# Third norm ahead of the matrix memory's norms, maxima of the second attention ahead of router, context mean and context sum

## What is computed

```
x = _layernorm(x + _L0_attn_ref(x, ...))            # first norm
x = _layernorm(x + _L0_xattn_ref(x, ctx, ctx, ...)) # matrix memory, a norm of its own inside; second norm
x = _layernorm(x + _L0_ffn_ref(x, ...))             # router, top 2 of 8 experts and a shared one; third norm
x = _layernorm(x + _L1_attn_ref(x, ...))            # second attention, 16 heads of width 8
x = _layernorm(x + _L1_xattn_ref(x, ctx, ...))      # uses the context's mean over the tokens
x = _layernorm(x + _L1_ffn_ref(x, ...))
```

## Time and profile before

| | |
|---|---|
| timed runs | 2484.64, 2486.62 and 2490.05 us; median 2486.62 |
| the profiled execution | 2482.89 us, of which 2481.2 are the span from first to last instruction |
| mean granted clock of PE | 0.901 of full speed |
| busy share of the span | PE 78%, DVE 68%, PEld 55%, ACT 45%, POOL 34% |
| chain that ended last | DVE 36%, PE 36%, issue 14%, POOL 6%, ACT 4%, DMA 2% |

### The profile page before, as it was taken

The page is one execution under the profiler, slowest core; times in us unless marked ns, Lnnn a source line. Parts: engine busy times, 40 slices in busy tenths (PEclk is TensorE's granted clock), DMA queues, the critical chain, the costliest instruction groups (busy, mean ns, idle before and its releaser), DMA issues.

```text
span 2481.2 us, 41883 instructions
## 1 busy us (share of the span) xinstructions
PE 1933.4 (78%) x14136; PEld 1373.1 (55%) x14136; DVE 1675.4 (68%) x3985; ACT 1113.2 (45%) x3168; POOL 842.6 (34%) x775
## 2 busy tenths in 40 slices
PE   2785697778886888678877888679877888775698
PEld 1464366645674457545664467546664567554354
DVE  8895894679656993669556993779466983713355
ACT  2462365335642465336642565246542564232234
POOL 0552462317420651226321651236321651211000
PEclk8997899889996999799997999799987999687699
DMA  4000012201040013101030203001120203051000
GB/s 136 1 1 9 15 54 64 64 18 61 5 121 12 28 41 93 42 13 58 23 105 11 68 1 114 21 15 56 56 71 11 69 1 118 10 200 61 9 13 21
DMA packets 72770, 117.35 MB, mean 47 GB/s; under 512 B 7822, under 2 KB 46870, under 8 KB 72038
## 3 DMA queue, kind: packets, MB, share of 16 engines
q1 hardware_dynamic: 67014, 101.42, 12.7%
q0 software_dynamic: 5536, 13.12, 1.8%
HBM read 95.18 MB, written 18.81 MB: 46 GB/s over the span
## 4 chain that ended last, share of the span: by engine, by line
DVE 36%; PE 36%; issue 14%; POOL 6%; ACT 4%; DMA 2%; DVEq 0%; SPq 0%; POOLq 0%; ACTq 0%
PE bank L1355 34%; DVE work L495 11%; DVE bank L504 5%; DVE work L513 3%; DVE work L493 3%; DVE max L794 2%; POOL hid L1263 2%; ACT work L952 2%; PE bank L1359 1%; POOL work L1231 1%; POOL work L1243 1%; DMA hid<-y_sorted,slot_id 1%; DVE acc L712 1%; ACT hid L952 1%; PE bank L1500 1%
## 5 line engine op out<-in xcount | busy, mean ns | idle before, releaser
L1355 PEld LDWEIGHTS bank<-work 128*128 128x128 f32 (+2 forms) x5152 | 389.6, 204 | 186.6 <-issue 146.6
L1355 PE MATMUL bank<-work 128*128 128x128 f32 (+2 forms) x5152 | 422.2, 312 | 69.3 <-DVE max L794 42.4
L952 ACT ACTIVATE work<-bank 128x512 f32<-128x512 f32 (+1 forms) x560 | 246.7, 516 | 317.1 <-PE bank L1355 264.8
L495 DVE TENSOR_TENSOR work<-bank,table_space 64x512 f32<-64x512 f32 x512 | 352.2, 688 | 6.8
L1231 POOL TENSOR_TENSOR work<-work 128x512 f32<-128x512 f32 x128 | 163.4, 1277 | 368.1 <-DVE work L495 267.7
L952 ACT ACTIVATE work<-work 128x512 f32<-128x512 f32 (+1 forms) x338 | 196.6, 618 | 166.8 <-DVE work L581 77.4
L952 ACT ACTIVATE work<-work,negmax 128x128 f32<-128x128 f32 x512 | 199.0, 390 | 100.2 <-DVE negmax L515 100.2
L1238 POOL TENSOR_TENSOR work<-sb_ident,nrm 128x512 f32<-128x512 f32 x128 | 133.2, 1041 | 275.4 <-ACT nrm L952 275.4
L1355 PE MATMUL bank<-work,table_space 128*128 128x512 f32 x256 | 140.4, 630 | 89.9 <-DVE negmax L515 59.4
L952 ACT ACTIVATE hid<-bank,w_ring 128x128 f32<-128x128 f32 x480 | 136.4, 370 | 162.9 <-PE bank L1355 162.8
L493 DVE TENSOR_TENSOR work<-bank,table_space 128x512 f32<-128x512 f32 x256 | 173.9, 679 | 45.2 <-PE bank L1355 19.2
(11 more groups left out here) (287 smaller groups left out, 3426.0 us busy)
## 6 DMA issues: line engine op xcount, KB each, us to landing
w_ring<-in_w_routed SPq DMA_DIRECT2D x120, 514.0 KB, 4.1
x_quad<-x_sorted SPq DMA_DIRECT2D x24, 256.0 KB, 2.9
y_sorted<-y_quad SPq DMA_DIRECT2D x24, 256.0 KB, 2.5
x_T<-in_x_T POOLq DMA_DIRECT2D x9, 256.0 KB, 3.1
x_row<-in_x_row POOLq DMA_DIRECT2D x9, 256.0 KB, 4.6
ctx_T<-in_ctx_T SPq DMA_DIRECT2D x8, 256.0 KB, 2.6
work<-in_ctx_row SPq DMA_DIRECT2D x8, 256.0 KB, 2.9
out<-act_row SPq DMA_DIRECT2D x8, 256.0 KB, 2.3
```

The lines of the kernel that those rows point to most:

```text
L495: last = v.tensor_tensor(rows(wk[i + 1][o]), rows(src[p]), sinT[o, s].unsqueeze(1).broadcast_to([DH0, GB, N]), ALU.mult)
L952: return nc.scalar.activation(o, i, f, **k)
L1355: return nc.tensor.matmul(o, l, r, start=start, stop=stop, skip_group_check=True)
```

## The change

On DVE the application of the third norm (`norm_t`) moves up, ahead of the product into `act_row[1]`; `scale_q2` moves ahead of the application of the second norm; the mean `cbc` and `context_sum` move behind `router_choice`; and `router_softmax` moves from ahead of `attn1` to behind the first four maxima. On ACT `t_to_T` moves ahead of the memory's norm and `mask_k2` ahead of the second norm. On PE the transposes of the third norm go to bank 6 and no longer to bank 3, which is still being read then; `wv2` waits for the statistics of the memory's norm (its bank 2 is free by then); and the transposes of `tok` and the router's logits move behind `scores2(0)`. POOL's and SP's programs stay as they are.

```diff
@@ DVE, xattn
                 link(v.reciprocal(rden[:], den[:]))
+                if d:
+                    dve.wait_ge(stored, g * 32 + 16)
+                    norm_apply(norm_t, g, 0, acc, act_row[0])
                 hr = act_row[1][:].rearrange("p b (h d) -> p b h d", h=H1)
...
                 norm_stats(norm_x, act_row[1])
-                if d:
-                    dve.wait_ge(stored, g * 32 + 16)
-                    norm_apply(norm_t, g, 0, acc, act_row[0])
                 norm_apply(norm_x, g, 1, act_row[1], resid_x, ahead=d)
...
-                norm(norm_x, g, 2, resid_x, tok, ahead=d)
+                norm_stats(norm_x, resid_x)
                 if d:
                     scale_q2(g)
+                norm_apply(norm_x, g, 2, resid_x, tok, ahead=d)
@@ DVE, attn1
-                v.tensor_scalar(cbc[:], csum[:].unsqueeze(2).broadcast_to([128, GB, N]), 1.0 / N, None,
-                                ALU.mult).then_inc(ctx_mean, 1)
-                if more:
-                    dve.wait_ge(ctx_mean, g + 1)
-                    context_sum()
-
...
                         v.tensor_reduce(max2[:, :, n, r], rows(ring2[(4 * n + r) % 6]), X, ALU.max).then_inc(mx2, 1)
+                    if n == 0 and more:
+                        router_softmax(g, 1)
...
                     router_choice(g, 1)
+                v.tensor_scalar(cbc[:], csum[:].unsqueeze(2).broadcast_to([128, GB, N]), 1.0 / N, None,
+                                ALU.mult).then_inc(ctx_mean, 1)
+                if more:
+                    dve.wait_ge(ctx_mean, g + 1)
+                    context_sum()
                     sort_tokens(g, 1)
@@ ACT, xattn
                     norm(norm_t, g, 0)
+                    t_to_T(g, 0, bank[6])
                 norm(norm_x, g, 1, ahead=d)
                 if d:
-                    t_to_T(g, 0, bank[3])
+                    mask_k2(g)
                 norm(norm_x, g, 2, ahead=d)
-                if d:
-                    mask_k2(g)
@@ PE, project2
-                transposes(bank[3], act_row[0], t_tr)
+                transposes(bank[6], act_row[0], t_tr)
...
+                if beside_norms:
+                    pe.wait_ge(norm_x.stats, g * LNS + LNS + 2)
                 for b in range(GB):
                     last = mm(rows(bank[2])[:, b], rows(seq_T)[:, b], res["wv2"][:], start=b == 0)
@@ PE, attn1
                 scores2(0)
+                if more:
+                    tokens_T(g, 1)
+                    router_logits(g, 1)
                 scores2(1)
```

More of the change, by code:

```diff
@@ L837, in _ @@
             xattn(0, 1)
-            router_softmax(0, 1)
             attn1(0, True)
@@ L843, in _ @@
                 xattn(g, 1)
-                router_softmax(g, 1)
                 attn1(g, True)
@@ L1178, in _ @@
             norm(norm_t, G - 1, 0)
-            t_to_T(G - 1, 0, bank[3])
+            t_to_T(G - 1, 0, bank[6])
             mask_k2(G - 1)
@@ L1615, in gate_tot_columns, with project2 @@
                 gate_columns(bank[0], gate[3], gate_T)
-            def project2(g):
+            def project2(g, beside_norms):
                 pe.wait_ge(norm_t.out, g * LNS + 1)
-                transposes(bank[3], act_row[0], t_tr)
+                transposes(bank[6], act_row[0], t_tr)
                 pe.wait_ge(t_T_sb, g * LNS + 1)
@@ L1655, in xattn, with tokens_T, router_logits @@
                         last.then_inc(num, 1)
-                if d:
-                    project2(g)
+            def tokens_T(g, d):
                 pe.wait_ge(norm_x.out, tally(g, d, LNS, 3))
                 transposes(bank[6], tok, x_tr)
+            def router_logits(g, d):
                 pe.wait_ge(x_T_sb, tally(g, d, 2, 2))
@@ L1785, in _ @@
             xattn(0, 0)
+            tokens_T(0, 0)
+            router_logits(0, 0)
             token_ranks(0, 0)
@@ L1790, in _ @@
             xattn(0, 1)
+            project2(0, True)
             attn1(0, 2, True)
@@ L1795, in _ @@
                 xattn(g, 1)
+                project2(g, True)
                 attn1(g, g + 2, True)
             heads_and_experts(G - 1, 1, False, True, True)
-            project2(G - 1)
+            project2(G - 1, False)
             attn1(G - 1, G, False)
```

## The result

The changed kernel takes 2493.97 us, median of 11 runs (2491.27 to 2497.9); the kernel before, beside it, 2487.73 (2483.95 to 2492.84, 11 runs). The ratio is 1.0025, with a 95% interval from 1.0016 to 1.0034: 6.2 us slower. The prediction drew the line between no change and slower at 0.2%; the median lies just past it, and the interval reaches to both sides of it. The profiled execution took 2491.27 us (span 2489.5, mean granted clock 0.898) against 2482.89 before (2481.2, 0.901).

A forecast was written before the change was run, and what follows sets the result against it. DVE's router, mean, sum and maxima set the stage's end, POOL's v2 chain 0.68 us behind; afterwards v2 binds. Net 0.12 us a group, 7 x 0.12 = 0.8 us, on the median 2486.62 gave 2487.4, range 2479 to 2495.

The forecast's parts named there:

- The bound after the change: Second scores: they wait for ACT's v2 copies behind POOL's memset and tok, no longer for maxima; 0.12 us later a group.
- the first rival, the clock: Behind the second scores PE's clock rises later in some groups (2495, chance 0.18) or earlier (2477, chance 0.08).
- the sum alone: Second scores 0.12 us later in each of seven groups, 0.8 us in all; bounds 0.4 to 2.8.
- The third rival, the maxima setting the pace: Second scores follow the earlier maxima and start 4.6 us sooner a group, 32 us in all: 2454; chance 0.05.
- Tok: Last norm's output on DVE, held by q2's scaling, ends 0.75 us later than before.
- Covers: ACT's seq_T and k2 copies end 0.22 and 0.14 us before the logarithms; mean and sum fit DVE's rank wait: cost 0.
- ACT's queue, the second rival: k2 copies ahead of the last norm's root delay tok by up to 2.40 us a group, 17 in all: 2504; chance 0.07.
- from ACT's end to PE's start: Between ACT's last v2 copy and PE's second scores: 0.05 us, within the 767.24 against 767.12 forecast for their start.
- more late rises: Behind the second scores three short groups turn long, 3 x 2.6 = 7.8 us, with the 0.8 2495; chance 0.18.

The follow-up runs named there:

- swapped waits: Changed kernel with PE's wait for the maxima put ahead of those for k2 and v2 before the second scores: 2494.26 us against 2487.2 for the kernel before.
- plain delay: Kernel before with two small DVE operations added ahead of the maxima of each group but the last: 2496.98 us against 2489.87.
- mean in front: Changed kernel with context mean and sum put back ahead of the maxima: 2496.91 us against 2489.87 for the kernel before.
- third norm alone: Kernel before with third norm, seq_T, q2, k2 and bank 6 edits only; mean, sum, router and maxima in old order: 2496.84 us against 2489.87.
- longest delay: Kernel before with four small DVE operations added ahead of the maxima of each group but the last: 2500.92 us against 2487.2, 4 runs.
- v2 cleared first, before: Kernel before with POOL's memset of v2 moved up behind a first quarter of moe_bias: 2486.56 us, ratio 0.9997.
- both edits: Kernel before with mean and sum behind the router's choice and POOL's memset of v2 behind a first quarter of moe_bias: 2447.33 us against 2488.17.

## Why the prediction was right and wrong

**The bound after the change: right.** The measured 2493.97 lies inside the range only because that took in the first rival, the clock; the sum alone was bounded at 2.8 us above before. The bound itself came as predicted. The prediction let the maxima off the path and put POOL's chain behind tok in their place. ACT's copies release the second scores, the maxima wait 5.67 us, and clearing v2 sooner takes the changed kernel to 1.1% below the kernel before and does nothing in the latter. The third rival, the maxima setting the pace, is out.

**Tok: right within 0.06 us.** Predicted 0.75 later, measured 0.81 (9.79 - 8.98). The bare root wait is the 0.60 that was read off the other norm, and tok stands right behind q2, as worked out. The third norm starts 0.48 us behind the reciprocal's start where `act_row` had stood 0.39 behind it; those 0.09 are more than the 0.06 left over. From tok to the end of the copies 7.22 us were measured for 7.23.

**Covers: right.** Seq_T ends 0.21 us ahead of its logarithm (755.16 to 755.37; predicted 0.22), k2 0.13 ahead of the other (759.74 to 759.87; predicted 0.14): ACT's queue, the second rival, is out. The mean takes 0.42 us in the idle time behind the choice. On its cost beside the memset (2.05 us) the Trainium skill has a rule (SBUF — State Buffer, section Who interferes with whom): `tensor_scalar` can take the port pair that VectorE shares with GpSimd, and whoever comes second is held until the other is done. The trace agrees: 0.42 with POOL idle, 2.05 beside its memset.

**The step that failed in the sum: from ACT's end to PE's start.** I took 0.05 us from another pair, seq_T to wk2. Here it was 0.25. Of the 0.20 more, 0.10 are the wait for the maxima, long met, that stands with its register instruction between the wait for v2 and the first matmul, as the swapped waits showed; the order of the instructions had it in plain sight. The other 0.10 are open. So the shift was 0.36 us a group and not 0.12: 0.12 + 0.06 + 0.20 = 0.38 by parts. Over seven groups that made 2.4 us, not 0.8. That alone is still under the 5 us that the prediction took for no change.

**The step that failed in the choice: the clock.** I gave the turn to more late rises 0.18, on the ground that the clock is low already where the second scores start and that the chain behind them is the same. Both are true, and the 8-us pieces show it: the stretches agree until their 16th microsecond. What differs is when the clock rises after that. That this goes by when the stretch begins is argued, not shown: groups 2 and 3 before run the same program and reach their second scores after the same 16.9 us, and take 29.02 and 31.61 us. Two of the three short groups turned long, 4.5 us over all stretches, nearly twice the 2.4 of the shift. The rival's working (2.6 us for each group that turns, slower from two on) was right in mechanism and size; two turned and not three, and the shift was larger. The mistake was to think of the clock as a coin apart from the sum: a small shift is enough to turn it. Nor is it a factor on the shift. Shifts of 0.26, 0.41, 0.49 and 0.81 us a group (waits swapped, plain delay, mean in front, third norm alone) each cost 7 us, the longest delay, of 0.83, cost 13.7 over four runs, one of 0.15 in six groups (v2 cleared first, before) cost nothing, and one of 0.43 the other way gained 18. The page TensorE: Matmul & The Clock Gate of the Trainium skill, section What's actually happening, has the window of activity run free of the kernel; stretches that begin alike and rise apart agree with it.

**Why not the gain that the edits hold.** Half of the change, mean and sum, gains 18 us by itself. The other half, the third norm's earlier application, makes tok 0.81 us later, and once the maxima are off the path tok is what counts. So the one half freed the path of the maxima, and the other made later what then bounds it.

**What stays open.** What sets the moment at which the clock falls and rises in a group, and so the bunch that its interval falls into; the other 0.10 us between copies and scores; and the price of the longest delay, 13.7 us over four runs, where the third norm alone cost 7.0 at the same shift.

## What to carry to other kernels

When two conditions end within less than a microsecond of each other, as the maxima and v2 did here, moving work that feeds both is judged by the one that is made later, so cost each chain to its last instruction, the waits and their register instructions among them. Where PE falls to its lower clock in every turn of a loop, as here, compare the times from turn to turn ahead of any sum: if they come in bunches, a shift of a few tenths of a microsecond costs nothing or a whole step. And the cheap gain was in a third queue: a memset of which only a quarter has to wait for tok, standing behind three adds.

## What was not expected of the hardware

- A shift of 0.41 us a group, 2.9 us in seven, cost 7 us, and one of 0.43 the other way gained 18; the stretch behind took 29.0 to 29.5 us or 31.0 to 31.8, with little between in most kernels.
- The idle time in front of PE's second scores did not tell their level: behind 1.53 and 1.62 us they ran at the higher (1.17 us), behind 0.57, 1.31, 3.65 and 4.88 at the lower (2.09 us).
- The time from one group's reciprocal to the next came in four bunches, near 269.8, 273.2, 276.5 and 279.8 us, in twelve kernels, whatever the shift.
- The router's subtraction on 128 x 32 values, both inputs in SBUF, ended 0.05 us behind the add that POOL had running beside it (the output bias after and before, the second add into `moe_bias` with both edits) in group 1 of three kernels: after at 764.71 + 0.80 = 765.51 for 764.20 + 1.26 = 765.46, in the kernel with both edits on the one before at 759.34 + 0.98 = 760.32 for 759.01 + 1.26 = 760.27, before at 763.17 for 763.12. The operation of that shape later in the router took 0.19 us.
- A wait that was long met, between the wait that came last and the matmul behind it, cost PE 0.10 us, in group 0 without and in the others with a register instruction.
